# Partial last row blocks as float32 column groups in a routed FFN, and the b2 addition on GpSimd

## The chip, the cores and the metric

One core of one Trainium2 chip runs the whole program. The metric is the device time of one execution in microseconds (us). Engines are named as in the profile: PE is TensorE, DVE is VectorE, ACT is ScalarE, POOL is GpSimd, SP is SyncE.

## The reference, cut to what matters

`x` has 8 x 256 = 2048 tokens of 256 values. Each token is rotated by small quaternion matrices, an 8-way router picks one expert for it, and that expert's gated FFN is added to the token.

```python
x_rot = _L0_cond_ref(x, ...)                    # 2048 x 256
top1  = argmax(softmax(x_rot @ router_w + router_b))
for i in range(8):
    h = x_rot @ w1[i] + b1[i]                   # 256 -> 2048
    a, g = split(h, 2)
    y = (a * sigmoid(g)) @ w2[i] + b2[i]        # 1024 -> 256
    out += where(top1 == i, y, 0)
return x + out
```

With the inputs of the reference the router gives the experts 0 to 7 these numbers of tokens: 308, 336, 181, 195, 258, 268, 327, 175. No expert has more than 512, so there is one tile per expert, eight in all, and no spare tile.

## The kernel before, in words

A prologue of some 37 us rotates the tokens, routes them, writes the rotated rows to `x_rows` in DRAM, and makes index lists and one control word per tile. The word holds a size class: the index in `SIZES` (L39) of the first size not smaller than the tile's count. The bodies of all engines branch on it.

Float32 products are made from float32r parts: a matrix is split in a high part (ACT copies it to float32r) and a low part (DVE subtracts), and hi*hi + hi*lo + lo*hi are three matmuls.

One tile i, with its engines:
- **POOL** (L456 to L474): when tile i is transposed it gathers the rotated rows of tile i+1 into `xg` (`gather`, four indirect DMAs, L417), scatters the four row blocks of tile i-1 to the output (`scatter`, L438; the first two wait for `y_done[0]`, the others for `y_done[1]`), and fetches the plain rows of tile i+1 into `y_out` (`fetch`, L429). It always does four blocks, however many the tile has. All is in one program order, so a wait holds up everything behind it.
- **SP** (L315 to L337, `load_tile`): the next tile's w1 (two DMAs of 1 MB) once all of this tile's w1 is split, then its w2 (two DMAs of 512 KB) once this tile's w2 is split.
- **PE** (L1147 to L1161): the first product (L1077, `first_product`), for each of the 8 hidden chunks c twelve matmuls (6 for the g half, 6 for the a half) over n columns, n being the size of the class, into a ring of three pairs of PSUM banks; then the transposes of tile i+1's gathered rows (L1054, `turn_held`, block 2 first where there is one); then the second product (L1122): for each block of 128 rows 24 matmuls of 256 columns (L1116 to L1118, `row_blocks`), in the order block 3, 2, 1, 0. Block 1 ends `outer_done`, block 0 ends `mm2_done`. It waits for `w2_split` at its start.
- **ACT** (L582, `gate_tile`): splits the transposed rows (L561), the four parts of w1 (L526), and in chunk c the sigmoid (L573) and the high part of the gated value of chunk c-1 (L579). The high part of w2 (L535) comes after chunk 2.
- **DVE** (L868, `gate_tile`): low parts of rows (L814) and w1 (L712), then for each c the gating (L821, into `u32`) and the low part of chunk c-1 (L827); after chunk 2 the addition of the previous tile's PSUM to `y_out` (`add_rows`, L850), after chunk 4 the low part of w2 (L717), after chunk 6 the addition of b2 to `y_out` (`add_b2`, L836).

ACT and DVE work over whole blocks (256, 384 or 512 columns). In the last tile `add_last` (L853) adds block 1 at `outer_done` and block 0 at `mm2_done`, and POOL scatters each as it is added (`end_blocks`, L475).

`u32`, the float32 gated value, is a ring of four chunks. `w2_raw`, the loaded w2, may be overwritten once split.

Of the kernel before, what the change touches and what calls it, by code (L numbers as in the profile page):

```python
# [5 lines left out]
def adaln_moe_ffn_kernel(nc, x, cond, q_right, gate, router_w, router_b, w1, b1, w2, b2, out):  # L6
# [32 lines left out]
    SIZES = (256, 288, 320, 352, 384, 512)  # L39
    BLOCKS = [(size + P - 1) // P for size in SIZES]  # L40
    SPARE = TOK // ITEM - 1
# [8 lines left out]
    LANDINGS = (0, 1, 2, 3, 5)  # L50
# [13 lines left out]
    with ctx:  # L64
# [20 lines left out]
        u32 = arena[:, SIG_RING * ITEM:8 * ITEM].rearrange("p (c t) -> p c t", c=8 - SIG_RING)  # L85
        x_t = sb("x_t", NB * DIM)[:, :].rearrange("p (k t) -> p k t", k=KH)
# [194 lines left out]

        def word_register(eng, name):
            return eng.alloc_register(name)
# [16 lines left out]
        def _(sp):  # L300
# [14 lines left out]
            def load_tile(i, e):  # L315

                for u in range(W1U):
                    sp.wait_ge(w1_split[u], i)
                for k in range(KH):
                    load_w1(e, k)  # L320
                for h in range(W2U):
                    sp.wait_ge(w2_split, i)
                    load_w2(e, h)
# [11 lines left out]
            sp.dma_start(b2_all[:, :], b2.rearrange("e d -> (e d)").partition_broadcast(P)).then_inc(b2_loaded, 16)  # L335
            for e in range(1, NE):
                load_tile(e, e)  # L337
# [3 lines left out]
            for i in range(NE, TAB):  # L341
                with sp.If(last_tile >= i):
                    load_tile(i, spare_expert(sp, i))

        @block.gpsimd
        def _(pool):
# [89 lines left out]

            def scatter_block(i, s):
# [18 lines left out]
            for i in range(NE):  # L456
# [14 lines left out]
                if i + 1 < NE:  # L471
                    if i + 1 >= YB:
                        wait_scattered(i + 1 - YB)
                    fetch(i + 1)  # L474
            def end_blocks(blocks):  # L475

                pool.wait_ge(last_added, 1)
                for s in range(1, min(blocks, 3)):
                    scatter_block(NE - 1, s)
                pool.wait_ge(last_added, 2)  # L480
                scatter_block(NE - 1, 0)
                if blocks == NSUB:
                    pool.wait_ge(last_added, 3)
                    scatter_block(NE - 1, 3)
# [18 lines left out]
        def _(act):  # L503
# [72 lines left out]
            def hi_u(i, c, n):  # L576

                act.wait_ge(pair_free[c], wrapped(c, i))
                nc.scalar.activation(u_hi[:, c * ITEM:c * ITEM + n], u32[:, c % (8 - SIG_RING), 0:n], ACT.Copy)\  # L579
                    .then_inc(u_hi_done, 1)  # L580

            def gate_tile(i, e, n):  # L582
# [4 lines left out]
                for c in range(NC):  # L587
# [3 lines left out]
                    if c == 2 and i < NE:  # L591
                        w2_hi_part(i)
# [8 lines left out]
            for e in range(NE):  # L601
                if_blocks(act, this_word(act, word_at), lambda blocks: gate_tile(e, e, blocks * P))
# [9 lines left out]
        def _(dve):  # L612
# [204 lines left out]
            def gated(i, e, c, n):  # L817
# [3 lines left out]
                V.scalar_tensor_tensor(u32[:, c % (8 - SIG_RING), 0:n], pair[c % RING][0][:, 0:n], b1_t[:, bass.ds(e * (2 * NC) + c, 1)],  # L821
# [367 lines left out]
```

## Time and profile before

| | us |
|---|---|
| median of the three runs | 216.72 |
| lowest and highest | 215.16 and 495.23 |
| the profiled execution, its own time | 216.05 |
| its span, from first to last instruction | 214.3 |
| around the span | 1.75 |
| mean granted TensorE clock | 0.988 |

Times in rows of the trace are us from the start of the span. A row of the timeline gives start, duration, engine, line, operation, output <- inputs, shape and count, and in brackets how long the engine was idle before it and what ended that. Matmuls overlap, so the time between two starts and not the duration is a matmul's cost. A float32 (not float32r) matmul with full products appears as two records.

### The profile page before, as it was taken

The numbers are of one execution on the slowest core, as the hardware profiler recorded it, in microseconds if no ns is written. First come the engines' busy times: TensorE is split into PE (matmuls) and PEld (weight loads), VectorE is DVE, ScalarE is ACT, GpSimd is POOL, SyncE is SP. The second block draws the span as 40 slices with busy tenths as digits, with TensorE's granted clock in tenths as the row PEclk, the third lists the DMA queues.
The fourth block names the chain that finished last, engine by engine and source line by source line (L and its number), as shares of the span: only waits on it lengthen the run. The fifth ranks groups of instructions, "written<-read, shape, count | busy, mean of one in ns | idle before, by whom it ended". The sixth has DMA issues, their size and how long they took to land.

```text
span 214.3 us, 4364 instructions
## 1 busy us (share of the span) xinstructions
PE 202.4 (94%) x1511; PEld 189.9 (89%) x1512; DVE 158.0 (74%) x308; ACT 122.2 (57%) x206; POOL 128.8 (60%) x163
## 2 busy tenths in 40 slices
PE   7999658999999999999999999999999999999992
PEld 3768524999999999999998999899999999999991
DVE  4839980589836997498889869994898469874960
ACT  2535841484918574567684868473939185745620
POOL 6004287775601878378778878887487818720752
PEclk9999997999999999999999999999999999999998
DMA  5994734979865174947499459827845691720011
GB/s 149 387 363 181 259 118 98 294 233 321 261 183 231 49 256 89 330 144 260 79 333 291 145 176 334 258 79 213 326 119 179 185 322 56 253 46 0 25 40 37
DMA packets 17540, 41.26 MB, mean 193 GB/s; under 512 B 2920, under 2 KB 11241, under 8 KB 15338
## 3 DMA queue, kind: packets, MB, share of 16 engines
q1 hardware_dynamic: 12784, 30.48, 40.0%
q0 software_dynamic: 4512, 10.50, 19.2%
q8 instruction: 7, 0.11, 0.2%
q14 instruction: 19, 0.16, 0.2%
q10 hardware_dynamic: 218, 0.01, 0.1%
HBM read 36.78 MB, written 6.03 MB: 200 GB/s over the span
## 4 chain that ended last, share of the span: by engine, by line
PE 65%; DVE 15%; issue 7%; POOL 6%; DMA 4%; ACT 3%; DVEq 0%; ACTq 0%
PE y_ps L1116 8%; PE y_ps L1117 8%; PE y_ps L1118 8%; PE g_ps L1096 6%; PE g_ps L1101 6%; PE g_ps L1097 5%; PE a_ps L1101 5%; PE a_ps L1097 5%; PE a_ps L1096 5%; DMA xg<-x_rows,g_idx 4%; PE y_ps L928 3%; DVE arena L821 3%; POOL out_dram L438 2%; POOL y_out L429 2%; DVE u_lo L827 2%
## 5 line engine op out<-in xcount | busy, mean ns | idle before, releaser
L438 POOL DMA_INDIRECT out_dram<-y_out,s_idx x30 | 44.0, 1465 | 42.5 <-DVE y_out L850 31.7
L573 ACT ACTIVATE arena<-g_ps,b_t 128x384 f32<-128x384 f32 (+1 forms) x64 | 34.5, 538 | 47.1 <-PE g_ps L1101 47.0
L821 DVE SCALAR_TENSOR_TENSOR arena<-a_ps,b_t,arena 128x384 f32<-128x384 f32 (+1 forms) x64 | 36.1, 563 | 31.2 <-PE a_ps L1101 28.4
L1116 PE MATMUL y_ps<-w_hi,u_hi 128*128 128x256 f32 x168 | 48.5, 289 | 0.1
L1117 PE MATMUL y_ps<-w_lo,u_hi 128*128 128x256 f32 x168 | 47.5, 283 | 0.0
L1118 PE MATMUL y_ps<-w_hi,u_lo 128*128 128x256 f32 x168 | 47.5, 283 | 0.0
L429 POOL DMA_INDIRECT y_out<-in_x_dram,g_idx x32 | 40.9, 1279 | 9.8 <-issue 9.8
L417 POOL DMA_INDIRECT xg<-x_rows,g_idx x32 | 36.5, 1141 | 14.9 <-issue 9.1
L579 ACT ACTIVATE u_hi<-arena 128x384 fp32r<-128x384 f32 (+1 forms) x64 | 30.7, 479 | 15.5 <-DVE arena L821 15.4
L712 DVE TENSOR_TENSOR w_lo<-w_raw,w_hi 128x1024 fp32r<-128x1024 f32 x32 | 37.2, 1221 | 1.8 <-ACT w_hi L526 1.4
L1096 PE MATMUL g_ps<-xr_hi,w_hi 128*128 128x256 f32 (+3 forms) x128 | 37.0, 302 | 0.6 <-ACT xr_hi L561 0.6
L1097 PE MATMUL a_ps<-xr_hi,w_lo 128*128 128x256 f32 (+3 forms) x128 | 36.6, 299 | 0.0
L1097 PE MATMUL g_ps<-xr_hi,w_lo 128*128 128x256 f32 (+3 forms) x128 | 36.6, 299 | 0.0
L1096 PE MATMUL a_ps<-xr_hi,w_hi 128*128 128x256 f32 (+3 forms) x128 | 36.5, 298 | 0.0
L1116 PEld LDWEIGHTS y_ps<-w_hi,u_hi 128*128 128x128 f32 x168 | 32.1, 191 | 0.8 <-DVE u_lo L827 0.5
L827 DVE TENSOR_TENSOR u_lo<-arena,u_hi 128x384 fp32r<-128x384 f32 (+1 forms) x64 | 31.9, 499 | 1.1 <-ACT u_hi L579 0.5
L1117 PEld LDWEIGHTS y_ps<-w_lo,u_hi 128*128 128x128 f32 x168 | 32.2, 191 | 0.0
L1118 PEld LDWEIGHTS y_ps<-w_hi,u_lo 128*128 128x128 f32 x168 | 32.1, 191 | 0.0
L526 ACT ACTIVATE w_hi<-w_raw 128x1024 fp32r<-128x1024 f32 x32 | 31.2, 1057 | 0.0
L1101 PE MATMUL g_ps<-xr_lo,w_hi 128*128 128x256 f32 (+3 forms) x128 | 28.1, 300 | 0.0
L1101 PE MATMUL a_ps<-xr_lo,w_hi 128*128 128x256 f32 (+3 forms) x128 | 27.9, 299 | 0.0
L1096 PEld LDWEIGHTS g_ps<-xr_hi,w_hi 128*128 128x128 f32 x128 | 24.2, 189 | 1.4 <-issue 1.2
(167 smaller groups left out, 295.6 us busy)
## 6 DMA issues: line engine op xcount, KB each, us to landing
w_raw<-in_L_ffn_w_dram SPq DMA_DIRECT2D x16, 1024.0 KB, 8.2
w_raw<-in_L_ffn_w_dram SPq DMA_DIRECT2D x16, 512.0 KB, 5.0
arena<-in_x_dram SPq DMA_DIRECT2D x4, 512.0 KB, 5.9
x_rows<-arena SPq DMA_DIRECT2D x8, 256.0 KB, 3.0
b_all<-in_L_ffn_b_dram SPq DMA_DIRECT2D x1, 1024.0 KB, 5.1
xg<-x_rows,g_idx POOLq DMA_INDIRECT x32, 6.4
y_out<-in_x_dram,g_idx POOLq DMA_INDIRECT x32, 4.4
out_dram<-y_out,s_idx POOLq DMA_INDIRECT x30, 3.7
```

Of the source, the lines that this page charges most:

```text
L417: nc.gpsimd.indirect_dma_start(out=xg[:, s * DIM:(s + 1) * DIM], out_offset=None, in_=x_rows, in_offset=bass.IndirectOffsetOnAxis(ap=g_idx ...
L429: nc.gpsimd.indirect_dma_start(out=y_out[i % YB][:, s * DIM:(s + 1) * DIM], out_offset=None, in_=x_flat, in_offset=bass.IndirectOffsetOnAx ...
L438: nc.gpsimd.indirect_dma_start(out=out_flat, out_offset=bass.IndirectOffsetOnAxis(ap=s_idx[:, i * NSUB + s:i * NSUB + s + 1], axis=0), in_ ...
L712: V.tensor_tensor(unit_of(w1_lo, u), raw_unit(u), unit_of(w1_hi[:, :].bitcast(F32), u), ALU.subtract)\
L821: V.scalar_tensor_tensor(u32[:, c % (8 - SIG_RING), 0:n], pair[c % RING][0][:, 0:n], b1_t[:, bass.ds(e * (2 * NC) + c, 1)], sig[:, c % SIG ...
L827: V.tensor_tensor(u_lo[:, at:at + n], u32[:, c % (8 - SIG_RING), 0:n], u_hi[:, at:at + n].bitcast(F32), ALU.subtract).then_inc(u_lo_done[c ...
L1096: T.matmul(dst, w_part(w1_hi, k), xh, start=(k == 0), stop=False)
L1097: T.matmul(dst, w_part(w1_lo, k), xh, start=False, stop=False)
L1101: last = T.matmul(dst, w_part(w1_hi, k), xr_lo[:, k * ITEM:k * ITEM + n], start=False, stop=(k == KH - 1))
L1116: T.matmul(dst, u_hi[:, uv], w2_hi[:, wv], start=first, stop=False)
L1117: T.matmul(dst, u_hi[:, uv], w2_lo[:, wv], start=False, stop=False)
L1118: last = T.matmul(dst, u_lo[:, uv], w2_hi[:, wv], start=False, stop=final)
```

## The change

- `SIZES` begins with 192 and loses 384. `PARTS` marks the sizes whose last block has 32 or 64 rows: 192 (block 1, 64 rows), 288 (block 2, 32 rows), 320 (block 2, 64 rows). With the counts above, tile 0 is a 320, tiles 2 and 7 are 192, tiles 4 and 5 are 288; tiles 1 and 6 (352) and tile 3 (256) have no such block. The first product still has at least 256 columns.
- Such a last block is computed by `part_block`: 8 float32 matmuls (one for each chunk) of `u32` against the unsplit `w2_raw`. The output is 64 or 32 partitions wide; chunk c writes to column group c mod 2 or c mod 4, so that two or four partial sums stand in different partitions of one bank. DVE adds them to the rows one after the other (`add_parts`): one more addition for 192 and 320, three more for 288.
- `u32` gets all 8 chunks (in the space of `x_t`), and `w2_raw` must last until `mm2_done`: the next w2 is loaded only after that, in SP's order ahead of the next but one w1.
- The order of the second product becomes block 3, 0, 2, 1; `outer_done` follows block 0, and the last tile's adds and scatters follow that order.
- `add_b2` for the eight expert tiles moves from DVE (2 or 3 blocks, after chunk 6) to POOL (always four blocks, 128 x 1024), as the last step of POOL's round, behind `fetch(i + 1)`.
- The high part of w2 goes from chunk 2 to chunk 4 on ACT, the low part from chunk 4 to chunk 5 on DVE.
- ACT and DVE take the widths 256, 288, 320, 384 or 512.

```diff
-    SIZES = (256, 288, 320, 352, 384, 512)
+    SIZES = (192, 256, 288, 320, 352, 512)
+    PARTS = {size: (size // P, size % P) for size in SIZES if size % P in (32, 64)}
...
+            def load_w2_again(i, e):
+
+                sp.wait_ge(w2_split, i)
+                sp.wait_ge(mm2_done, i)
                 for h in range(W2U):
                     load_w2(e, h)
...
+            load_w1_again(1, 1)
             for e in range(1, NE):
-                load_tile(e, e)
+                load_w2_again(e, e)
+                if e + 1 < NE:
+                    load_w1_again(e + 1, e + 1)
...
+            def add_b2(i):
+
+                pool.wait_ge(x_fetched[i % YB], (i // YB + 1) * NSUB * 16)
+                if i == 0:
+                    pool.wait_ge(b2_loaded, 16)
+                rows = y_out[i % YB][:, :].rearrange("p (s d) -> p s d", s=NSUB)
+                nc.gpsimd.tensor_tensor(rows, rows, b2_all[:, i * DIM:(i + 1) * DIM].unsqueeze(1).to_broadcast([P, NSUB, DIM]),
+                                        ALU.add).then_inc(b2_added, 1)
...
                     fetch(i + 1)
+                add_b2(i)
...
-                    if c == 2 and i < NE:
+                    if c == 4 and i < NE:
                         w2_hi_part(i)
...
+                    with dve.If(f_size(word) == SIZES.index(left[0])):
+                        rows = y_out[i % YB][0:wide, s * DIM:(s + 1) * DIM]
+                        for g in range(1, P // wide):
+                            link(V.tensor_tensor(rows, y_ps[1][g * wide:(g + 1) * wide, PLACE[s] * DIM:(PLACE[s] + 1) * DIM],
+                                                 rows, ALU.add))
...
-                    if c == 4 and i < NE:
+                        add_rows(i - 1, word_before)
+                    if c == 5 and i < NE:
                         w2_lo_part(i)
...
-                    if c == 6:
+                    if c == 6 and i >= NE:
                         add_b2(i, e, blocks)
...
+            def part_block(size, at1, at2, done=None):
+
+                s, wide = PARTS[size]
+                groups = P // wide
+                for c in range(NC):
+                    pe.wait_ge(pair_free[c], at2 if c >= CARRIED else at1)
+                    g = c % groups
+                    last = T.matmul(y_ps[1][g * wide:(g + 1) * wide, PLACE[s] * DIM:(PLACE[s] + 1) * DIM],
+                                    u32[:, c, s * P:s * P + wide], w2_raw[:, c * DIM:(c + 1) * DIM],
+                                    start=c < groups, stop=c >= NC - groups)
+                if done is not None:
+                    last.then_inc(done, 1)
...
-                row_blocks((1,), at1, done=outer_done)
-                row_blocks((0,), at1, done=mm2_done)
+                with pe.Else():
+                    with pe.If(f_size(word) == SIZES.index(320)):
+                        part_block(320, at1, at2)
+                    with pe.If(f_size(word) == SIZES.index(288)):
+                        part_block(288, at1, at2)
+                with pe.If(f_size(word) == SIZES.index(192)):
+                    part_block(192, at1, at2, done=mm2_done)
+                with pe.Else():
+                    row_blocks((1,), at1, done=mm2_done)
```

## Rows read from the trace of the kernel before

**Rows 1.** The page's busy times, share of the span and instruction counts.
```profile
PE 202.4 (94%) x1511; PEld 189.9 (89%) x1512; DVE 158.0 (74%) x308; ACT 122.2 (57%) x206; POOL 128.8 (60%) x163
```
**Rows 2.** The page's chain that ended last, shares of the span by engine.
```profile
PE 65%; DVE 15%; issue 7%; POOL 6%; DMA 4%; ACT 3%; DVEq 0%; ACTq 0%
```
**Rows 3.** Timeline of PE, tiles 3 to 7, at first product, transposes, second product.
```profile
115.95 0.33 PE L1054 MATMUL a_ps<-ident,xg 128*128 128x128 f32 x1 [0.42 <-DMA xg<-x_rows,g_idx]
...
122.65 0.37 PE L1096 MATMUL g_ps<-xr_hi,w_hi 128*128 128x288 f32 x1
...
135.62 0.32 PE L1054 MATMUL a_ps<-ident,xg 128*128 128x128 f32 x1
...
145.46 0.37 PE L1096 MATMUL g_ps<-xr_hi,w_hi 128*128 128x288 f32 x1
...
158.38 0.32 PE L1054 MATMUL a_ps<-ident,xg 128*128 128x128 f32 x1
...
168.20 0.40 PE L1096 MATMUL g_ps<-xr_hi,w_hi 128*128 128x352 f32 x1
...
192.72 0.30 PE L1096 MATMUL g_ps<-xr_hi,w_hi 128*128 128x256 f32 x1
...
204.25 0.28 PE L1116 MATMUL y_ps<-w_hi,u_hi 128*128 128x256 f32 x1
```
**Rows 4.** Timeline of POOL from tile 2 to tile 5: first DMAs of its rounds.
```profile
91.89 1.02 POOL L438 DMA_INDIRECT out_dram<-y_out,s_idx  x1 [3.86 <-DVE y_out L850]
...
94.53 2.60 POOL L438 DMA_INDIRECT out_dram<-y_out,s_idx  x1 [0.30 <-issue]
...
105.75 1.00 POOL L417 DMA_INDIRECT xg<-x_rows,g_idx  x1 [0.30 <-issue]
...
108.36 1.00 POOL L417 DMA_INDIRECT xg<-x_rows,g_idx  x1 [0.31 <-issue]
...
125.54 1.00 POOL L417 DMA_INDIRECT xg<-x_rows,g_idx  x1 [0.30 <-issue]
...
145.23 1.00 POOL L417 DMA_INDIRECT xg<-x_rows,g_idx  x1 [0.30 <-issue]
...
152.44 1.02 POOL L438 DMA_INDIRECT out_dram<-y_out,s_idx  x1 [2.29 <-DVE y_out L850]
```
**Rows 5.** The chain in order of time: start, us, what, around tile 4's gather.
```profile
108.36 7.54 DMA xg<-x_rows,g_idx
```
**Rows 6.** The gathers' line: time from issue to landing.
```profile
DMA to landing us min/median/max: 2.9/6.4/8.1
```
**Rows 7.** Groups by form: second product's matmuls and DVE's b2 additions, three-block tiles.
```profile
L1116 PE MATMUL y_ps<-w_hi,u_hi 128*128 128x256 f32 x168 | 48.5, 289 | 0.1
...
L836 DVE TENSOR_TENSOR y_out<-y_out,b_all 128x768 f32<-128x768 f32 x5 | 4.7, 949 | 0.0
```
**Rows 8.** Timeline of PE: the router's float32 products in four column groups.
```profile
12.16 1.07 PE L980 MATMUL a_ps<-x_t,wr_rot 128*32 128x256 f32 x16
13.11 1.07 PE L980 MATMUL g_ps<-x_t,wr_rot 128*32 128x256 f32 x16
```
**Rows 9.** Groups by form: two-input operations on POOL in the prologue.
```profile
L407 POOL TENSOR_TENSOR of_token<-oh,sm 128x128 f32<-128x128 bf16 x1 | 0.4, 403 | 0.1
...
L410 POOL TENSOR_TENSOR of_token<-of_token 128x64 f32<-128x64 f32 x1 | 0.4, 373 | 0.1
...
L410 POOL TENSOR_TENSOR of_token<-of_token 128x32 f32<-128x32 f32 x1 | 0.3, 309 | 0.1
```
**Rows 10.** Timelines of ACT and DVE in the last tile: w2's two parts.
```profile
197.21 1.90 ACT L535 ACTIVATE w_hi<-w_raw 128x2048 fp32r<-128x2048 f32 x1
...
201.04 2.28 DVE L717 TENSOR_TENSOR w_lo<-w_raw,w_hi 128x2048 fp32r<-128x2048 f32 x1
```
**Rows 11.** DMA issues by line: w2's loads, count, size each, us to landing.
```profile
w_raw<-in_L_ffn_w_dram SPq DMA_DIRECT2D x16, 512.0 KB, 5.0
```
**Rows 12.** Timeline of DVE: the last addition.
```profile
210.26 0.42 DVE L863 TENSOR_TENSOR y_out<-y_ps,y_out 128x256 f32<-128x256 f32 x1 [2.37 <-PE y_ps L1118]
```

## The prediction: what the change does to the time

> **What bounds the kernel now.** I read the busy times first: PE works 94% of the span, POOL 60% [rows 1]. A reader would say PE-bound, and the chain agrees at first sight: 65% PE [rows 2]. But 6% is POOL and 4% DMA, so somewhere PE is not the limit. PE's timeline shows where: tile 4's transposes at 115.95 waited 0.42 us for a gather [rows 3]. POOL's timeline shows why. POOL last waited for another engine at 91.89 (3.86 us, for DVE); from there its DMAs follow each other with gaps of 0.3 us until 150, and only at 152.44 does it wait again (2.29 us) [rows 4]. Its rounds begin at 105.75, 125.54 and 145.23: 19.8 and 19.7 us each, filled to the brim. A share of 60% over the span hides a stretch of 58 us in which POOL has no slack. Tiles 2 and 3 are short (two row blocks), and POOL does four blocks of gather, scatter and fetch for them all the same. So through tiles 2 to 5 PE and POOL run neck and neck; in tiles 0, 1, 6 and 7 PE is alone.
>
> **PE's gain.** The second product of the last tile starts at 204.25 and its 48 matmuls end some 0.28 us before DVE's addition at 210.26 [rows 3, 12]: 5.73 / 48 = 0.12 us a matmul, 2.87 us for a block of 24. There are 168 x 3 such matmuls, 21 blocks [rows 7]; five of them change. A changed block is 8 float32 matmuls of 256 columns. The router's products have this very form with 32 columns in four groups, 8 matmuls as 16 records, and the second set starts 0.95 us behind the first [rows 8]. So a 288's block costs 0.95: it saves 1.92, in tiles 4 and 5. Groups of 64 columns are not in the trace. Two at a time instead of four: 0.95 x 2 = 1.90, saving 0.97. Ends: 0.95 (they go like the narrow ones), and 0.95 x 4 = 3.80 (no overlap, 0.93 lost). I take 1.90, the value half the groups give. It applies to tiles 0, 2 and 7. Sum on PE alone: 2 x 1.92 + 3 x 0.97 = 6.75 us.
>
> **What is put on POOL.** DVE loses 8 additions, up to 0.95 us each [rows 7]; that is worth nothing by itself where PE waits for a gather. POOL gets 8 additions of 1024 elements with two inputs. Its own rows are small: 309 ns for 32, 373 for 64, 403 for 128 elements [rows 9]. Slope from 32 to 64: 2.0 ns an element; from 64 to 128 (bf16 inputs, another form): 0.47. So 1024 elements cost 0.37 + 960 x 2.0 = 2.3 us, or at the low end 0.40 + 896 x 0.47 = 0.8 us. I take 2.25 plus 0.15 behind it, b = 2.4 us a round, since the float32 rows have the form of the new one. The Trainium skill, page "GPSIMD Engine Reference", section "Elementwise — side-by-side cycle accounting", gives 4497 ns for a float32 addition of 2048, which by half would be an estimate of 2.25; no run here shows one yet.
>
> **The race between POOL and PE, tile by tile.** Tile 0 ends 0.97 earlier, so tile 2 starts and POOL's scatter at 91.89 comes 0.97 earlier. b2 of tile 1 falls into the slack ahead of it (3.86). From there the chain is POOL's:
> - Gather for tile 4 starts at 105.75 - 0.97 + b; the third DMA, which PE needs first, 2.61 later, and lands 7.54 after its issue [rows 4, 5]: 114.9 + b = 117.3. PE was ready at 115.53 before and is now ready at 115.53 - 0.97 - 0.37 = 114.2 (0.37: tile 2 saves 0.97 less 0.6 of w2 lateness, below). It waits 3.1 us. Tile 4 starts 6.70 after its transposes (122.65 - 115.95): 124.0.
> - The next gather begins 19.79 + b later, third DMA 2.8 on, landing taken at the line's median 6.4 [rows 6], since the w1 load that shares the queues is then further behind: 138.6. PE is ready 12.97 after 124.0 (135.62 - 122.65): 137.0. Wait 1.6. Tile 5 starts 9.84 - 1.92 = 7.92 on: 146.5 (before: 145.46).
> - The third round likewise: 19.69 + b, landing 160.5; PE ready at 146.5 + 12.92 = 159.4. Wait 1.1. Tile 6 starts 7.90 on: 168.4 (before: 168.20).
> Tile 6 is long and its second product unchanged; POOL catches up there. So of the 5.8 us saved in tiles 0 to 5, nothing is left at tile 6. In a formula: tile 6 starts at 161.2 + 3b. Each us of the addition costs three, once in each saturated round.
>
> **w2's new place.** The next w2 load waits for `mm2_done`, the tile's start, and lands about 5.0 + 0.5 us into it [rows 11]. ACT took w2 at 197.21 - 192.72 = 4.49 us into the last tile [rows 3, 10]; two chunks later (2 x 12 x 0.12 = 2.88) is 7.37. So the load has 1.9 us to spare; if the w1 load behind it slows it beyond that, every us over is a us late. DVE's low part then follows the high part (1.90), a sigmoid, a gating and a low part. Between the starts of the two parts lay 3.83 before; at least 1.9; I take 3.2, so it ends at 7.37 + 3.2 + 2.28 = 12.85. PE asks for it at 204.25 - 192.72 = 11.53: 1.3 us late in the last tile (0 to 2.0). In tile 2, 0.6 of the same remains, as transposes stand between. Tiles 4 and 5 hide it behind the gather's wait; in the long tiles 0, 1 and 6 it is in time. This is not seen by POOL's chain.
>
> **The other edits.** Narrower ACT and DVE work (288 for 384) shortens chains that are no longer last: 0. Three more additions of 32 partitions in tiles 5 and 6 fall into DVE's idle time; `y_done[0]`, for which POOL waits first, is given ahead of them: 0. In the last tile one addition more, like the 0.42 us of [rows 12] and a semaphore, 0.47 us, stands at the very end. POOL's b2 of tile 7 comes behind `scatter(6)`, ends before block 1 is done: 0, but see the rival. Deeper branches: up to 0.3 a tile on ACT and DVE, behind the second product.
>
> **Sum.** From tile 6's start to the end of the span it was 214.3 - 168.20 = 46.1. Now + 1.3 - 0.97 + 0.47 = 46.9. Span 168.4 + 46.9 = 215.3, and with 1.75 around it 217.0. The profiled execution took 216.05 and the median is 216.72: no change that can be told. About 2% (4.3 us, below 212.4 or above 221.1) is what a measurement of this kernel can tell.
>
> **Rivals.**
> - **The addition is cheap on POOL** (0.97 us with its gap). The slope of the third row speaks for it, the float32 rows against. Then gathers are hardly late: tile 4 at 122.6, tile 5 at 143.6, tile 6 at 164.4; span 164.4 + 46.9 = 211.3, time 213.1. Even at b = 0 PE alone gives tile 6 at 163.3 and 212.0; without lateness of w2 it falls to 210.1.
> - **POOL and DVE shut each other out** (slower). One of POOL's scatters took 2.60 us where its neighbour took 1.02 [rows 4], while DVE's two-input w2 subtraction ran; a 2.25 us addition, placed where DVE subtracts w1 and w2, may wait 1.6 us for one. Then b = 4.0, gathers land at 118.9, 141.8, 165.3; tile 6 starts at 173.2, span 220.1, time 221.9. It decides from b = 2.07 (where 161.2 + 3b + 46.9 is the old span) and passes 2% at b = 3.8. Against it: only one or two issues in a round were stretched like this. The rule behind it is in the Trainium skill, "SBUF — State Buffer", section "Who interferes with whom": a DVE instruction with two SBUF inputs contends with a GpSimd instruction that reads SBUF. The stretched scatter is in line with contention, though a descriptor-writing DMA is not the case that it names.
> - **64-column groups do not overlap.** Tiles 0 and 7 each lose 1.90 against the forecast (tile 2's loss is inside the gather's wait): time 220.8. The narrow groups did overlap [rows 8], which speaks against it.
>
> **Chances.** Forecast 0.52, cheap addition 0.22, lock-out 0.16, no overlap 0.10. The forecast with its ends (b 1.7 to 3.1 moves 2.1 us either way, w2 0 to 2.0) covers 214 to 219.5. With the rivals the range is 210.5 to 222.0. Faster by 2% takes the cheap case where w2 is in time too, and a tail of the forecast: 0.20. Slower by 2%: about half of the lock-out and of the no-overlap cases and a tail: 0.17. Within 2%: 0.63.
>
> **What would show it.** Right: PE waits of 1 to 4 us at L1054 for the gather in tiles 3, 4 and 5; POOL with no wait on DVE from tile 2 to tile 5 and rounds of 22 us; the addition at 2.2 us; tile 6 starting near 168; the 288 blocks 0.95, the 64-wide ones 1.9 us; w2's low part ending 12.9 us into a 192 tile. Wrong: tile 6 starting at 163 to 165, or an addition under 1.5 us, means the cheap case; additions over 3 us, or DVE subtractions stretched beside them, the lock-out; part blocks of 3.8 us the third. If w2 lands later than 7.4 us into the tile, the sum is too low in each tile.

## The result, and the profile after

The changed kernel took 243.94 us (median of 4 runs, 240.0 to 244.43), the kernel before beside it 215.94 us: a ratio of 1.123, 95% interval 1.114 to 1.132. It is slower by 28 us. Medians here and below are of all executions; the intervals and ratios leave out those that took over 1.5% more than the fastest of their kernel. The forecast was no change that can be told (217.0), and the range ended at 222.0. The profiled execution took 243.54 us; its span is 241.8 against 214.3.

From the page of the changed kernel, the busy times and the clock that TensorE was granted in 40 slices:

```profile
PE 205.5 (85%) x1471; PEld 186.8 (77%) x1472; DVE 165.3 (68%) x309; ACT 119.2 (49%) x206; POOL 146.3 (61%) x171
PEclk9999799999999999979999799999889999999587
```

PE's share fell from 94% [rows 1] to 85%: PE waits now. Where, the time by stage says. These are the stretches from one tile's first product to the next, tiles 3 to 7 (the last one up to PE's end), first of the changed kernel, then of the kernel before:

```profile
core 0: us, PE busy (x) PEld busy (x) DVE busy (x) ACT busy (x) POOL busy (x), PEclk, DMA share, GB/s
109.85:132.33 22.48, 18.66 (x150) 18.02 (x150) 17.20 (x27) 12.72 (x23) 18.59 (x14) 1.00 0.67 204
132.33:156.98 24.65, 22.30 (x166) 21.14 (x166) 17.23 (x26) 13.01 (x23) 18.76 (x14) 0.93 0.54 171
156.98:182.45 25.47, 22.47 (x166) 21.09 (x166) 17.02 (x29) 13.28 (x23) 20.51 (x16) 0.93 0.59 185
182.45:210.99 28.54, 25.06 (x173) 24.60 (x173) 23.98 (x31) 14.31 (x23) 14.43 (x11) 1.00 0.51 149
210.99:234.20 23.21, 18.54 (x138) 17.32 (x136) 12.21 (x20) 8.10 (x17) 7.37 (x6) 0.85 0.19 61
```

```profile
103.84:122.65 18.81, 18.34 (x153) 17.96 (x151) 16.16 (x27) 12.72 (x23) 15.46 (x12) 1.00 0.75 231
122.65:145.46 22.81, 22.65 (x174) 22.07 (x175) 19.85 (x28) 14.42 (x23) 18.54 (x15) 1.00 0.65 202
145.46:168.20 22.74, 22.63 (x175) 22.08 (x175) 18.31 (x26) 14.42 (x23) 16.79 (x14) 1.00 0.63 203
168.20:192.72 24.52, 24.52 (x174) 24.50 (x173) 18.05 (x26) 14.32 (x23) 13.63 (x11) 1.00 0.59 183
192.72:210.30 17.58, 17.50 (x146) 17.29 (x144) 10.73 (x22) 8.06 (x17) 7.35 (x5) 1.00 0.07 23
```

Every tile is longer, by 3.7, 1.8, 2.7, 4.0 and 5.6 us; 6.0 us were lost before tile 3, and 3.5 come after the last product. In the last column but two the granted clock is below 1.00 in three of the stages. PE worked at the lower of its two levels (1.2 GHz) in four stretches: some 3.5 us each from 101.7, 132.4 and 173.5, and 4.4 us up to 231.7. Each follows a wait of PE, of 1.52, 2.19, 1.47 and 4.64 us; behind the wait of 1.68 us at 109.85 the clock stayed high. At the lower level the last tile's matmuls start 0.21 us apart, against 0.12 before and after:

```profile
231.10 0.41 PE L1189 MATMUL y_ps<-w_hi,u_lo 128*128 128x256 f32 x1
231.32 0.39 PE L1187 MATMUL y_ps<-w_hi,u_hi 128*128 128x256 f32 x1
```

So of some 15 us of work at the lower level 6 to 7 us are lost to it (an estimate: 15 x (1 - 0.12 / 0.21)). That is one reason why PE's busy time rose (205.5 us) although it has less to compute.

Who is waited for, from the changed kernel's waits (engine, line, releaser: us in total, times, longest):

```profile
POOL out_dram L474 <- DVE y_out L908: 35.1, 7, 12.9
PE y_ps L1187 <- DVE w_lo L755: 12.6, 7, 4.6
PE g_ps L1167 <- DVE w_lo L750: 6.0, 4, 2.2
PE y_ps L1187 <- DVE u_lo L865: 3.5, 3, 2.0
```

In the tiles PE waits for DVE alone: 12.6 us for w2's low part (L755), in each of tiles 1 to 7; 6.0 us for w1's low part (L750) at four starts; 3.5 for `u_lo`. No wait for a gather is left, and POOL waits for DVE in seven of its eight rounds (before: five, 31.7 us). The saturated POOL of the forecast does not exist in this kernel: what is late is DVE. PE's waits, 22.1 us, and the tail, 3.5 us, make 25.6 of the 27.5 us of span; with the 6 to 7 us of the lower clock the sum is 32, which leaves 4 to 5 us for what PE saved.

The sized terms were right. The five changed blocks on PE and the addition on POOL:

```profile
56.74 1.95 PE L1200 MATMUL y_ps<-w_raw,x_t 128*64 128x256 f32 x16
151.67 1.07 PE L1200 MATMUL y_ps<-w_raw,x_t 128*32 128x256 f32 x16
```

```profile
L470 POOL TENSOR_TENSOR y_out<-y_out,b_all 128x1024 f32<-128x1024 f32 x8 | 19.1, 2392 | 0.2
```

From its start to the next row block the 64-wide block takes 1.88 us (58.62 - 56.74) and the 32-wide one 1.00 (forecast 1.90 and 0.95); the addition takes 2.39 us (forecast 2.25). By half of the Trainium skill's figure ("GPSIMD Engine Reference", "Elementwise — side-by-side cycle accounting") the estimate was 2.25; the trace is 6% above it.

**The last tile in rows.** First DVE, then POOL, then ACT, then PE, of the changed kernel:

```profile
218.76 0.48 DVE L859 SCALAR_TENSOR_TENSOR x_t<-a_ps,b_t,arena 128x256 f32<-128x256 f32 x1 [1.24 <-DVEq L884]
222.37 2.44 DVE L865 TENSOR_TENSOR u_lo<-x_t,u_hi 128x256 fp32r<-128x256 f32 x1
224.73 2.28 DVE L755 TENSOR_TENSOR w_lo<-w_raw,w_hi 128x2048 fp32r<-128x2048 f32 x1
```

```profile
222.14 2.37 POOL L470 TENSOR_TENSOR y_out<-y_out,b_all 128x1024 f32<-128x1024 f32 x1
```

```profile
219.28 0.42 ACT L617 ACTIVATE u_hi<-x_t 128x256 fp32r<-128x256 f32 x1 [1.14 <-DVE x_t L859]
219.60 1.90 ACT L573 ACTIVATE w_hi<-w_raw 128x2048 fp32r<-128x2048 f32 x1
```

```profile
227.31 0.58 PE L1187 MATMUL y_ps<-w_hi,u_hi 128*128 128x256 f32 x1 [4.64 <-DVE w_lo L755]
```

The tile starts at 210.99. DVE's queue stands still for 1.24 us at the branches of `add_parts` (L884), a gating is late, ACT waits for it, and w2's high part starts 8.61 us into the tile (forecast 7.37). Then POOL's addition runs from 222.14 to 224.51, and the `u_lo` subtraction that starts beside it at 222.37 takes 2.44 us where its neighbours take 0.42. The low part ends 16.0 us into the tile (forecast 12.85), and PE has waited 4.64 us for it (forecast 1.3).

### The profile page after: what moved, and what is told of

It is laid out like the page before. It is cut to its first block and busy times, and to the rows that moved or that the text cites. A ratio compares the mean times of both kernels' runs of the same rounds, so it can differ in the third digit from the quotient of the medians.

```text
span 241.8 us, 4370 instructions
## 1 busy us (share of the span) xinstructions
PE 205.5 (85%) x1471; PEld 186.8 (77%) x1472; DVE 165.3 (68%) x309; ACT 119.2 (49%) x206; POOL 146.3 (61%) x171
## 5 line engine op out<-in xcount | busy, mean ns | idle before, releaser
L474 POOL DMA_INDIRECT out_dram<-y_out,s_idx x30 | 30.5, 1016 | 51.9 <-DVE y_out L908 35.1
L859 DVE SCALAR_TENSOR_TENSOR x_t<-a_ps,b_t,arena 128x256 f32<-128x256 f32 (+3 forms) x64 | 33.8, 530 | 32.7 <-PE a_ps L1172 18.3
L611 ACT ACTIVATE arena<-g_ps,b_t 128x256 f32<-128x256 f32 (+3 forms) x64 | 32.6, 509 | 47.5 <-PE g_ps L1172 47.5
L1187 PE MATMUL y_ps<-w_hi,u_hi 128*128 128x256 f32 x128 | 40.1, 313 | 16.2 <-DVE w_lo L755 12.6
L444 POOL DMA_INDIRECT xg<-x_rows,g_idx x32 | 42.9, 1339 | 12.2 <-issue 8.6
L617 ACT ACTIVATE u_hi<-x_t 128x256 fp32r<-128x256 f32 (+3 forms) x64 | 29.0, 453 | 33.3 <-DVE x_t L859 33.1
L750 DVE TENSOR_TENSOR w_lo<-w_raw,w_hi 128x1024 fp32r<-128x1024 f32 x32 | 44.4, 1444 | 1.4 <-ACT w_hi L564 1.0
L1188 PE MATMUL y_ps<-w_lo,u_hi 128*128 128x256 f32 x128 | 38.5, 300 | 0.0
L1189 PE MATMUL y_ps<-w_hi,u_lo 128*128 128x256 f32 x128 | 38.4, 300 | 0.0
L865 DVE TENSOR_TENSOR u_lo<-x_t,u_hi 128x256 fp32r<-128x256 f32 (+3 forms) x64 | 37.0, 578 | 1.3 <-ACT u_hi L617 0.3
L564 ACT ACTIVATE w_hi<-w_raw 128x1024 fp32r<-128x1024 f32 x32 | 31.2, 1056 | 1.1 <-issue 1.1
```

Of the source, the lines that this page charges most:

```text
L444: nc.gpsimd.indirect_dma_start(out=xg[:, s * DIM:(s + 1) * DIM], out_offset=None, in_=x_rows, in_offset=bass.IndirectOffsetOnAxis(ap=g_idx ...
L611: nc.scalar.activation(sig[:, c % SIG_RING, 0:n], pair[c % RING][1][:, 0:n], ACT.Sigmoid, bias=b1_t[:, bass.ds(e * (2 * NC) + (NC + c), 1) ...
L750: V.tensor_tensor(unit_of(w1_lo, u), raw_unit(u), unit_of(w1_hi[:, :].bitcast(F32), u), ALU.subtract)\
L859: V.scalar_tensor_tensor(u32[:, c, 0:n], pair[c % RING][0][:, 0:n], b1_t[:, bass.ds(e * (2 * NC) + c, 1)], sig[:, c % SIG_RING, 0:n], ALU. ...
L865: V.tensor_tensor(u_lo[:, at:at + n], u32[:, c, 0:n], u_hi[:, at:at + n].bitcast(F32), ALU.subtract).then_inc(u_lo_done[c], 1)
L1187: T.matmul(dst, u_hi[:, uv], w2_hi[:, wv], start=first, stop=False)
```

## The experiments

All edits are against the changed kernel unless said otherwise. In two of the four sets the kernel before took 229.2 and 228.3 us on the chip given, in the two others 215.1 and 215.0. So runs are compared within their set, by us or by their ratio to the kernel before. The changed kernel stood beside the kernel before twice, here (1.123) and in the second set (1.139), not in the first and third.

**First set: one part undone at a time** (kernel before: 229.18 us).

`e1_b2_on_dve`: `add_b2` back from POOL to DVE at chunk 6.

```
-                    if c == 6 and i >= NE:
+                    if c == 6:
                         add_b2(i, e, blocks)
```

> The changed kernel with the additions of b2 back on DVE after chunk 6 (2 or 3 blocks), all else as changed. Theory 1 (POOL's addition shuts DVE out): the trace of the changed kernel has DVE's two-input operations beside the eight additions stretched by 2.0 to 2.8 us each; PE's waits that follow from them are 1.56 in tile 0, about 1.5 each at the first products of tiles 3, 4 and 5, 2.0 in tile 6 and about 2.5 in tile 7, some 10 to 11 us, so the time falls from 243.5 to 231 to 235; the low parts of w1 go back to 1.22 us each and no low part of u takes over 0.6. Theory 2 (the gaps of 2.3 to 2.8 us at the start of a tile on ACT and DVE set the pace, and the shut-out is mostly hidden in them): the time falls by 5 us at most, to 238 to 241, and PE still waits for w1's low part. Theory 3, my forecast's (POOL's round is too long): gathers would be late without being so now; the changed trace has no wait for a gather, so a fall by 3 us a round is not expected.

243.85 us, ratio 1.062.

`e2_w2_early`: w2's parts back to chunks 2 and 4 (`if c == 4 and i < NE: w2_hi_part(i)` becomes `c == 2`, `c == 5` for the low part becomes `c == 4`).

> The changed kernel with the high part of w2 back after chunk 2 and the low part after chunk 4, all else as changed (w2 still loaded only at the tile's start). Theory 1 (the later place makes w2's low part the last thing before the second product): PE's waits for it, 0.87, 1.52, 1.44, 1.17, 1.47, 1.49 and 4.64 us in tiles 1 to 7, go to nearly 0 in tiles 1 to 6 and to 1 to 2 us in the last, some 9 us; time 233 to 236. Theory 2 (what PE does not wait for at w2 it waits for at the next w1 part, since DVE's chain is as long in any order): the fall is 3 us or less, and the waits for w1's low part grow by what those for w2 lose. ACT takes w2 at 5.5 us into a tile instead of 4.5, so a sigmoid is up to 1 us late; that costs PE nothing with three PSUM pairs.

238.32 us, ratio 1.039.

`e3_three_widths`: ACT and DVE bodies for 256, 384 and 512 columns, as before the change.

```
-            widths = (2 * P, 288, 320, 3 * P, ITEM)
+            widths = (2 * P, 3 * P, ITEM)
```

> The changed kernel with ACT and DVE bodies for 256, 384 and 512 columns only, as before the change (the 288 and 320 tiles are worked on as 384), all else as changed. Theory 1 (the five nested bodies per tile cost a fetch of instructions at each tile: gaps of 2.3 to 2.8 us on ACT in three tiles and on DVE in three, 0.2 to 0.6 before): the gaps go to under 0.8 us, PE's waits for the low part of w1 fall from 5.9 us to 2 or less; the wider operations cost 0.1 us each, hidden; time 236 to 240. Theory 2 (the gaps come from add_parts' branches and the second word register, or from elsewhere): the gaps stay and the time is 243 to 246, the wider operations making it no better.

252.57 us, ratio 1.092.

`e4_groups_alone`: all three undone; the column groups, the kept w2 and its load behind `mm2_done` remain. This kernel is called the base below.

> All three undone at once: b2 on DVE, w2 parts after chunks 2 and 4, three widths. What is left of the change is the column groups with their additions, the new block order, and w2 loaded only at the tile's start. Theory 1 (the three causes are separate and make up all of the loss): PE's gain of 6.75 us less small losses shows, 208 to 213 against 216 before. Theory 2 (keeping w2 unsplit costs by itself: load late, additions of the groups, bigger DVE code): 216 to 222. If the three single undoings sum to much more than this one's fall, they share waits.

231.54 us, ratio 0.998, 95% interval 0.993 to 1.003.

If the parts add up, three differences to the base give three prices: late w2 and widths 12.3 us (e1), b2 and widths 6.8 (e2), b2 and late w2 21.0 (e3). Solved: late w2 13.3, b2 on POOL 7.8, widths -1.0. But the base's ten executions lie at 227.9 to 230.4 (four) and 231.5 to 236.4, and e3's at 249.7, 250.9, 254.3 and 255.3. By the lower ones, which the ratios use (base 228.4, e3 250.3), the same sums give 13.7, 8.2 and 1.7. All this rests on adding up, so the third set adds each part alone.

**Second set: w2's place and buffer, and b2 alone** (kernel before: 215.11 us).

`f1_changed_again`: the changed kernel itself.

> The changed kernel itself, so that it stands beside the variants and the kernel before on one chip: in the runs so far the kernel before took 216 us in one call and 229 in another, so times of different calls can't be set beside each other, only ratios. Expected: a ratio of 1.10 to 1.13. If the ratio follows the chip, the loss is in something that differs between the chips (transfers, instruction fetch); if it stays at 1.12, it is in the order of the work.

246.32 us, ratio 1.139 (1.130 to 1.148).

`f2_groups_w2_at_3`: the base with w2's high part behind chunk 3 instead of 2.

> As the run with all three undone (b2 on DVE, three widths, w2 loaded only at the tile's start), but the high part of w2 after chunk 3 instead of 2; the low part after chunk 4. In that run ACT waited up to 3.7 us for the load of w2 and PE 1.2 to 1.9 us at the transposes of five tiles, behind DVE's gating of chunk 5. Theory 1 (w2's late load is the price of keeping it unsplit): one chunk later, 1.4 to 1.9 us, ACT no longer waits for it, PE's waits at the transposes fall below 0.7, and the ratio to the kernel before falls from 1.00 to 0.97 or 0.98. Theory 2 (DVE's and ACT's own chain is what is late, wherever w2 stands): the ratio stays at 0.99 to 1.01 and the waits move to the start of the second product.

219.59 us, ratio 1.018 (1.013 to 1.023). Both theories' ratios were missed; the base stood at 0.998 on the chip of the first set and stands at 1.023 on that of the third.

`f3_groups_two_w2`: the base with two buffers for w2, so that its load need not wait for the second product; PE picks the buffer by the tile's parity.

```
-        w2_raw = sb("w2_raw", W2U * UNIT)
+        w2_raws = [sb(f"w2_raw{b}", W2U * UNIT) for b in range(2)]
...
-                sp.wait_ge(mm2_done, i)
+                if i > 1:
+                    sp.wait_ge(mm2_done, i - 1)
```

> As the run with all three undone, but with two buffers for the loaded w2, so that it is loaded as early as before the change (after the last tile's split, behind w1), and the unsplit copy still stands for the part blocks. High part after chunk 2, low part after chunk 4. Theory 1 (the late load is what remains): ACT waits for w2 nowhere after tile 0, the waits at the transposes go to 0 to 0.4, and PE's gain of 6.75 us comes through but for POOL's rounds, which were filled before: ratio 0.970 to 0.985. Theory 2 (POOL's gather or DVE's added work is the next bound at once): ratio 0.99 to 1.01, with waits for the gather at the transposes of tiles 4 and 5.

217.92 us, ratio 1.013 (1.008 to 1.018), above both theories' ratios. The best of the versions, and still not faster than the kernel before on this chip. In the base (g1 below) ACT stands 0.4 to 2.6 us ahead of w2's high part in each of tiles 1 to 7, 7.9 us in all; with two buffers that is gone (one such wait in e4, 1.76 us, names the load). So the late load of the one kept w2 is a part of the base's loss.

`f4_b2_on_pool_alone`: the kernel before with `add_b2` moved to POOL and nothing else.

> The kernel before with one part of the change: the eight additions of b2 by GpSimd behind the fetch. All else as before. Theory 1 (the additions shut out DVE's two-input operations, and before the change w1's low part had little room): DVE's w1 parts beside them are stretched by 2 us, PE waits 1 to 2 us in most tiles for w1 or the low part of u; ratio 1.03 to 1.05, and the TensorE clock falls below 0.98. Theory 2, my forecast's (POOL's rounds grow by 2.4 us, three of them saturated, gathers late): ratio 1.02 to 1.03 with waits for the gather at the transposes of tiles 4, 5 and 6. Theory 3 (both hidden): 1.00.

219.19 us, ratio 1.011 (1.003 to 1.018), between the ratios of theory 3 (1.00) and theory 2 (1.02 to 1.03). The race of the forecast can be looked at here, without w2 and groups in the way. Its waits:

```profile
POOL out_dram L447 <- DVE y_out L859: 14.1, 2, 12.2
DVE y_out L867 <- POOL y_out L443: 5.4, 1, 5.4
PE a_ps L1063 <- DVE arena L832: 1.3, 1, 1.3
```

POOL is full from 93 to 195 (it waits for DVE twice, before: five times), as the forecast had it, and its rounds begin at 109.05, 130.10, 152.85 and 175.60, 21.1, 22.8 and 22.8 us apart (forecast 22.2 and 22.1). Still PE waits for no gather: only 1.3 us in tile 4, at the transposes, for a gating of DVE. Forecast were 3.1, 1.6 and 1.1 us in tiles 3, 4 and 5 (2.8, 1.5 and 0 by the same sum without the shorter blocks, which this kernel has not). What made the difference is the landing. PE needs the third DMA of a gather; it was issued at 111.91, 132.85 and 155.61, and PE's transposes started at 116.92, 137.79 and 160.55, so each landed within 5.0 us or so, where the forecast had 7.54 and 6.4. The page has the median of all gathers at 4.0 us, before 6.4:

```profile
xg<-x_rows,g_idx POOLq DMA_INDIRECT x32, 4.0
```

Why they land sooner is open. The span grew by 3.9 us (218.2 for 214.3) in two other places. In tile 0 a `u_lo` subtraction beside POOL's first addition takes 3.27 us (its neighbours 0.55), and the second product 10.37 us instead of 8.81. At the end POOL's last addition stands behind `scatter(6)`, which begins only at 205.95, and DVE waits 5.4 us for it before it may add the last tile's rows: from PE's end to the span's end 6.2 us instead of 4.1. The forecast had put that place at 0.

**Third set: each part added to the base** (kernel before: 214.99 us).

`g1_base_again`: the base. `g2_base_plus_b2_on_pool`, `g3_base_plus_late_w2` and `g4_base_plus_five_widths`: the base with that one part as in the changed kernel.

> The kernel with all three undone once more, as the base for the three runs beside it, each of which puts one of the three back. On a chip where the kernel before takes 215 to 216: ratio 1.00 to 1.02 by the run with w2 after chunk 3 (1.018 there); PE's waits at the transposes 1 to 2 us in tiles 3 to 6.

220.18 us, ratio 1.023 (1.019 to 1.028).

> Base plus b2 on GpSimd (three widths, w2 after chunks 2 and 4). Theory 1 (the shut-out costs where DVE has no slack, and the group kernels have less of it than the kernel before, where the same addition cost 1.05%): 3 to 6% over the base, w1's low parts of 2.3 us and more beside an addition, PE waiting for them. Theory 2 (the cost is that of the kernel before): 1% over the base.

228.48 us, ratio 1.059 (1.053 to 1.065): 8.3 us for b2 on POOL.

> Base plus the later place of w2's two parts (high after chunk 4, low after chunk 5). Theory 1: the wait moves from the transposes to the start of the second product, 1.2 to 1.5 us a tile as in the changed kernel; since the base waits as long for w2's load, 0 to 1.5% over the base. Theory 2 (this is the main part of the loss): 4 to 5% over the base.

233.99 us, ratio 1.087 (1.082 to 1.091): 13.8 us for the late w2.

> Base plus the five bodies for a tile on ACT and DVE. Theory 1 (instruction fetch at the jumps): gaps of 2 to 3 us on ACT or DVE at the start of several tiles that the base does not have; hidden behind the second product in part, 2 to 4% over the base. Theory 2 (narrower operations relieve DVE, the gaps are hidden): 1 to 2% under the base, since 288 and 320 for 384 saves DVE 1.6 us in tiles 4 and 5.

225.2 us, ratio 1.044 (1.036 to 1.051): 5.0 us for the five widths.

Base 5.2, b2 8.3, w2 13.8 and widths 5.0 make 32.3 us above the kernel before; the changed kernel stands 28.0 above it in one set and 31.2 in another, and was not run in this one. So the parts are enough for all of it, and to 4 us or so they add up. Two prices agree with the first set's to 0.5 us (7.8 or 8.2, and 13.3 or 13.7); the widths' does not (-1.0 or 1.7 there), and that stays open.

*b2.* DVE's subtractions by shape, the base and then the base with b2 on POOL (count | busy, mean ns of one | idle before):

```profile
L749 DVE TENSOR_TENSOR w_lo<-w_raw,w_hi 128x1024 fp32r<-128x1024 f32 x32 | 37.1, 1221 | 1.6 <-ACT w_hi L563 1.0 <-issue 0.3
L864 DVE TENSOR_TENSOR u_lo<-x_t,u_hi 128x384 fp32r<-128x384 f32 x40 | 22.1, 552 | 0.6
L864 DVE TENSOR_TENSOR u_lo<-x_t,u_hi 128x256 fp32r<-128x256 f32 x24 | 10.0, 418 | 0.5 <-ACT u_hi L616 0.5
L873 DVE TENSOR_TENSOR y_out<-y_out,b_all 128x768 f32<-128x768 f32 x5 | 4.8, 952 | 0.0
L873 DVE TENSOR_TENSOR y_out<-y_out,b_all 128x512 f32<-128x512 f32 x3 | 2.1, 688 | 0.0
```

```profile
L750 DVE TENSOR_TENSOR w_lo<-w_raw,w_hi 128x1024 fp32r<-128x1024 f32 x32 | 48.7, 1580 | 1.2 <-ACT w_hi L564 0.7 <-issue 0.3
L865 DVE TENSOR_TENSOR u_lo<-x_t,u_hi 128x384 fp32r<-128x384 f32 x40 | 24.8, 620 | 0.7
L865 DVE TENSOR_TENSOR u_lo<-x_t,u_hi 128x256 fp32r<-128x256 f32 x24 | 12.9, 536 | 0.6 <-ACT u_hi L617 0.5
```

The same subtractions cost DVE 11.6 + 2.7 + 2.9 = 17.2 us more, 2.15 us for each of the eight additions; DVE got rid of 6.9 us of additions for it. In the trace a train of four w1 subtractions takes 6.84 us beside an addition of POOL and 4.63 in the one tile where none runs beside it. The Trainium skill's rule ("SBUF — State Buffer", "Who interferes with whom": a port pair shared by GpSimd and DVE's second input, locked by one at a time) fits: it is DVE that stands still for nearly all of POOL's instruction. Of the price of 8.3 us a part lies elsewhere, behind the last scatter (see the end). The two-buffer kernel with b2 on POOL was not run.

*w2.* The base with the late w2, its waits:

```profile
PE y_ps L1188 <- DVE w_lo L754: 10.9, 7, 2.3
```

Seven waits for w2's low part: 0.87 to 1.59 us in tiles 1 to 6, 2.31 in the last. The forecast had this wait in the 192 tiles only. Tile 6, a long one, shows why it is in the long ones too; it starts at 180.59. ACT, then DVE:

```profile
191.98 0.53 ACT L616 ACTIVATE u_hi<-x_t 128x384 fp32r<-128x384 f32 x1 [1.83 <-DVE x_t L858]
192.41 1.90 ACT L572 ACTIVATE w_hi<-w_raw 128x2048 fp32r<-128x2048 f32 x1
```

```profile
189.59 1.33 DVE L891 TENSOR_TENSOR y_out<-y_ps,y_out 32x256 f32<-32x256 f32 x3 [0.64 <-DVE y_out L912]
191.33 0.62 DVE L858 SCALAR_TENSOR_TENSOR x_t<-a_ps,b_t,arena 128x384 f32<-128x384 f32 x1 [0.41 <-DVE y_out L891]
195.88 2.29 DVE L754 TENSOR_TENSOR w_lo<-w_raw,w_hi 128x2048 fp32r<-128x2048 f32 x1
```

ACT comes to w2 behind the `u_hi` of chunk 3, and waits 1.83 us for its gating (191.33), which stands on DVE behind the additions of the tile before: 187.67 to 190.92, with the three of the groups and their gaps. So w2's high part starts 11.8 us into the tile, the low part ends at 198.17, and PE was ready at 196.86. Without the 1.83 it would, by this sum, have been in time. So the wait in the long tiles is w2's place together with DVE's additions just ahead, those of the groups among them; no run has the late place without the groups. The 10.9 us of waits are less than the price of 13.8: the mean granted clock is 0.969 here, 0.991 in the base.

*Widths.* The waits of the base with five bodies, then the rows of the base that answer to the first two:

```profile
DVE xr_lo L851 <- issue: 12.0, 4, 5.8
ACT xr_hi L598 <- issue: 8.4, 5, 2.8
PE g_ps L1168 <- DVE w_lo L749: 5.9, 3, 3.1
```

```profile
DVE xr_lo L851 <- issue: 0.5, 1, 0.5
ACT xr_hi L598 <- issue: 1.0, 4, 0.4
```

Between tiles ACT stands for 1.7 us and DVE for 3.0 us on average, up to 5.8, with nothing that they wait for: their first instruction of a new body is issued late. With three bodies ACT loses 0.25 us there and DVE 0.5 once. The queue that carries instructions (q14 on the page) moved 33 packets instead of the base's 22. That the gap is the fetch of the chosen body is my reading; what the runs show is that it comes with the two bodies more. It does so on the first set's chip too, in e1 (ACT up to 3.0 us in five gaps, DVE 2.5 to 5.4 in four), where the differences gave the widths next to no price.

**Last set: why the groups alone bring nothing** (kernel before: 228.3 us, 23 runs). TensorE should save 6.75 us, yet f3 is 1.3% slower than the kernel before.

`h1_no_group_sums`: f3's kernel without `add_parts`.

```
-                if word is not None:
-                    add_parts(i, word, list(PARTS))
```

> The kernel of f3 (three widths, b2 on DVE, w2 in two buffers) without the additions that bring the groups' partial sums together: DVE adds the first group alone, so this leaves out part of the second product's sum. Theory (DVE's chain is what eats TensorE's gain): the additions cost DVE 2.1 us behind a 288 tile and about 1 us behind a 192 tile, ahead of gatings for which TensorE waits, so about half of their 7 us goes off the time: 2.5 to 4 us below f3, that is 213 to 215.5 us beside a kernel before of 215. Rival (the additions lie in idle time, as the prediction had it, and something else in the rebuilt kernel costs the rest): within 0.7 us of f3.

225.07 us (218.6 to 227.1).

`h2_groups_64_alone`: f3's kernel with `PARTS` for sizes with 64 odd rows only; `part_block(288, ...)` becomes `row_blocks((2,), at1)`.

> The kernel of f3 with groups for the 64-row blocks alone; the two 288 tiles compute their third block in full, as before the change. TensorE gives back 2 x 1.9 us, DVE is relieved of 2 x 2.1 us. Theory (DVE's chain): the two cancel, within 1 us of f3. Rival (DVE's additions are hidden): 3 to 4 us above f3.

230.37 us, ratio 1.005 (1.001 to 1.009).

`h3_no_groups`: f3's kernel with full row blocks everywhere and no `add_parts`.

> The kernel of f3 with no column group and no addition for one: every block in full, all else (order of the blocks, u32 in x_t, two w2 buffers, registers, sizes) as in f3. Theory: TensorE does all its work again, 6.75 us more than in f3, and DVE's chain is as short as before the change, so the time is that of the kernel before within 1 us if the scaffold costs nothing, and f3 stands at about +1.3% with the groups. Rival (the scaffold itself costs): 3 us or more above the kernel before, and then the groups do bring a part of their gain.

229.03 us (225.1 to 230.9).

`h4_groups_two_w2_again`: f3's kernel.

> The kernel of f3 once more, on the same chip as the three others of this set, since two chips differed by 6% in the time of the kernel before: 1.013 of the kernel before, as in f3, within 0.5%.

227.46 us, ratio 0.994 (0.991 to 0.997). The 0.5% that was expected around 1.013 was missed: on this chip the kernel before lost 13 us and this one 10.

Within the set, by medians: no groups 229.0, groups 227.5, groups without their sums 225.1, groups for the 64-wide blocks alone 230.4. But the executions lie far apart: h3's six at 225.1 and 228.6 to 230.9, h4's twelve at 225.5 to 229.5, h1's six at 218.6, 221.6 and 224.9 to 227.1, h2's twelve at 225.6 to 228.4 (four) and 229.6 to 231.8. What stands is the direction of h1: without the sums the kernel is faster, by 2.4 us in the medians (2.5 to 4 was expected), and by 7 if its two lowest are set against h4's nine lowest. So the additions do not lie in idle time. What does not stand is the rest: the scaffold's cost is +0.7 us by medians and -3.2 by h3's one low execution, the groups bring 1.6 us with their sums or nothing, and h2 is 2.9 above h4 by medians, near the rival's 3, but 0.8 by its lowest four, within the 1 us of the theory. Where the sums cost is seen at the transposes, first with the sums (h4), then without (h1):

```profile
103.60 0.33 PE L1125 MATMUL a_ps<-ident,xg 128*128 128x128 f32 x1 [0.60 <-DVE x_t L857]
123.11 0.41 PE L1125 MATMUL a_ps<-ident,xg 128*128 128x128 f32 x1 [1.89 <-DVE x_t L857]
144.76 0.32 PE L1125 MATMUL a_ps<-ident,xg 128*128 128x128 f32 x1 [0.68 <-DVE x_t L857]
168.02 0.32 PE L1125 MATMUL a_ps<-ident,xg 128*128 128x128 f32 x1 [1.86 <-DVE x_t L857]
218.61 1.73 PE L1207 MATMUL y_ps<-w_raw,x_t 128*64 128x256 f32 x14 [0.66 <-issue]
```

```profile
121.93 0.32 PE L1122 MATMUL a_ps<-ident,xg 128*128 128x128 f32 x1 [1.84 <-DVE x_t L857]
169.19 1.07 PE L1204 MATMUL y_ps<-w_raw,x_t 128*32 128x256 f32 x16 [0.43 <-issue]
```

Waits of 0.6, 0.7 and 1.9 us for the gating of the last chunk go with the sums (the one in tile 3 stays). And the rows with "issue" show what became of PE's own saving: a part block behind a branch starts 0.3 to 0.7 us late. From PE's timeline, second product start to the next tile's first product (tile 7: to PE's end), in us:

| tile | before | base (g1) | saved | forecast |
|---|---|---|---|---|
| 0 | 8.81 | 8.25 | 0.56 | 0.97 |
| 2 | 5.86 | 5.36 | 0.50 | 0.97 |
| 4 | 9.22 | 7.62 | 1.60 | 1.92 |
| 5 | 9.19 | 7.84 | 1.35 | 1.92 |
| 7 | 5.97 | 5.97 | 0.00 | 0.97 |

4.0 us of 6.75: the blocks are as short as forecast, and some 0.3 to 1.0 us a tile is lost around them, 0.3 to 0.7 of it in the gaps in front of them where the rows show one; that the rest is branches too is my reading. In f3, whose PE also branches on the buffer, 2.3 are left. Against them stand 6.3 us of waits at the base's transposes (before: 0.42), 0.8 in the first product of tile 2, and 1 us more at the end.

## Why the prediction was wrong, by its own steps

- **"What is put on POOL", "The race between POOL and PE"**: the addition's size was right (2.39 for 2.25), and its effect wrong. The step that failed is that POOL's rounds, filled before, would bind PE through the gathers. Alone (f4) the rounds grew as forecast, to 22.8 us, but a gather's third DMA landed within 5.0 us or so instead of the 7.54 and 6.4 taken over from before. In the changed kernel the rounds have slack again, since PE's tiles are longer. The forecast counted what POOL does and took DVE's subtractions as untouched.
- **The lock-out rival** named the contention and put it on the wrong side: POOL was to wait for DVE. POOL's additions took 2.37 to 2.63 us, so hardly longer; DVE's took 2.15 us more for each. Its own sign, DVE subtractions stretched beside an addition, came true; its sum did not, as it went by POOL's rounds. Price 8.3 us in g2 against the rival's 4.9 (221.9 - 217.0). The stretched scatter [rows 4] was the hint, and I read it as a cost to POOL alone.
- **"w2's new place"**: 1.3 us late in the last tile, 0.6 in tile 2, "in time" in tiles 0, 1 and 6, hidden in 4 and 5. Measured: late in all of tiles 1 to 7, 12.6 us in the changed kernel, 13.8 us of time by itself (g3). This is the largest miss. Two steps failed: that w2's high part starts when its chunk is due (in the long tile read above ACT came to it 1.8 us late, for a gating behind the groups' sums), and that the gather's wait, which never came, hides it in tiles 4 and 5. In the last tile the term of 1.3 became 4.6: the high part started 1.24 us later behind the branches of `add_parts`, and from its start to the low part's went 5.13 us instead of 3.2, 2.0 of these the lock-out.
- **"The other edits"**: deeper branches were given up to 0.3 us a tile and called hidden. They cost 1.7 us on ACT and 3.0 on DVE at a tile's turn, ahead of w1's low part, for which PE then waits (6.0 us in the changed kernel, 5.0 us of time in g4). A new branch was priced as an instruction, without a row that shows one of five bodies; the "issue" rows of the kernel before, 0.2 to 0.6 us, were of three bodies.
- **The three more additions in "DVE's idle time"**: their cost is 2.4 us or more (h4 against h1), and with the branches' gap DVE's chain to the last gating is the one that PE waits for at the transposes. DVE was busy 16 to 20 us of each 19 to 25 us stage, tiles 3 to 6; I called the rest idle without following where it lies.
- **"PE's gain"**: the blocks' durations were right to 0.05 us. Summing them to 6.75 was not: 4.0 us arrived. And the sum had no term for the granted clock: in the changed kernel PE's waits brought the lower level with them, for an estimated 6 to 7 us.
- **"POOL's b2 of tile 7 ... 0"**: held in the changed kernel (224.51, long before the last block), not in f4, where DVE waits 5.4 us for it.
- **Right**: the sizes of block and addition; groups of 64 overlap two at a time, so the third rival was out; less work on PE is not the end of the matter when its suppliers are near the limit. Only, the supplier was DVE.

## What to carry to other kernels

Where one engine is at 94% and another at 75%, price every edit by the longest chain of the second engine to the next thing the first one asks for, in every tile, not by busy shares; "hidden" must name a row. Moving an elementwise operation with two SBUF inputs from DVE to POOL does not relieve DVE while DVE has two-input operations of its own: here 6.9 us were taken off and 17.2 put on. And each body more in a per-tile branch has a price at the place where the branch is taken, to be measured before it is traded for narrower work.

## What the runs showed that was not expected

- POOL's addition of 128x1024 float32 stops DVE's subtraction with two SBUF inputs for 2.0 to 2.2 of its 2.4 us (0.42 to 2.44 us in the row above), and the addition itself is hardly slowed.
- Choosing among five bodies instead of three leaves gaps of up to 2.8 us on ACT and 5.8 us on DVE with no releaser; where the kernel before takes 229 us the same gaps stand in the trace (e1), and the price by differences is -1.0 to 1.7 us instead of 5.0.
- Chips differ by 6% on the kernel before, and not evenly: of the 9.0 us by which h4's span exceeds that of the same kernel in f3, 6.1 lie in the first product of tile 0 (20.5 us for 14.4), where PE waits for DVE's gatings; why those are late is open. And the groups' kernel with two w2 buffers is 1.3% slower than it on one and 0.6% faster on the other. A gain below 2% should not be believed from one chip.
- After the last scatter is issued the changed kernel's span goes on for 5.0 us, the kernel before for 2.4 and f3's for 2.6. The base has 2.5, g2 5.1, g4 4.7: so 2.6 of b2's 8.3 us and 2.2 of the widths' 5.0 lie there, behind all waits of PE. Why, no run here tells.
